# Shifted-window attention block on one core: projections over 128 rows with zero-padded weights, and q and k parts moved straight from tile to tile

## The reference

```python
y = roll(layernorm(x) * w1 + b1, (-3, -3)); win = 7x7 windows of y     # 2048 windows of 49 tokens, 64 channels
q, k, v = split(win @ qkv_w.T)                                          # 8 heads of 8 channels
attn = softmax(q @ k.T * 8**-0.5 + bias + mask)                         # 49 x 49 per window and head
out = (attn @ v) @ proj_w.T + proj_b                                    # windows back, roll back
x = x + out
z = layernorm(x) * w2 + b2
return x + gelu(z @ fc1_w.T + fc1_b) @ fc2_w.T + fc2_b                  # hidden width 256
```

## Time and profile before

| | |
|---|---|
| three timed runs | 2358.63, 2359.13, 2376.8 us (median 2359.13) |
| profiled execution | 2345.75 us, span 2343.9 us |
| mean granted TensorE clock | 0.986 |
| PE, PEld busy | 95%, 72% of the span |
| DVE, ACT, POOL busy | 75%, 66%, 76% |
| DMA | 217.73 MB, mean 93 GB/s; data queue 43.2% of 16 engines |

### The profile page before, as it was taken

How to read it: one execution, slowest core, us unless ns; L and a number is a source line. 1 busy time by engine, 2 the same in 40 slices (tenths; PEclk the granted TensorE clock), 3 DMA queues, 4 the chain that set the end, 5 groups by cost and what they waited for, 6 DMA issues and landing times.

```text
span 2343.9 us, 155989 instructions
## 1 busy us (share of the span) xinstructions
PE 2217.1 (95%) x66852; PEld 1699.0 (72%) x66852; DVE 1756.3 (75%) x3230; ACT 1548.0 (66%) x2435; POOL 1770.1 (76%) x1687
## 2 busy tenths in 40 slices
PE   5999999999999999999999999999999999999997
PEld 4777777777777777777777777777677777777775
DVE  5787787777777877777777777777777777777774
ACT  4567666666666776766666766666666666666765
POOL 5787787777777877776777777777777777777774
PEclk7999999999999999999999999999999999999999
DMA  5444444444444454444444444444444444444541
GB/s 122 98 92 103 91 94 100 87 90 90 95 97 90 96 100 90 99 90 85 96 87 92 102 89 93 103 93 90 94 90 89 93 91 97 94 91 93 103 87 41
DMA packets 137659, 217.73 MB, mean 93 GB/s; under 512 B 29336, under 2 KB 95114, under 8 KB 137114
## 3 DMA queue, kind: packets, MB, share of 16 engines
q1 hardware_dynamic: 137114, 208.95, 43.2%
HBM read 131.69 MB, written 77.15 MB: 89 GB/s over the span
## 4 chain that ended last, share of the span: by engine, by line
PE 85%; ACT 6%; issue 5%; DMA 1%; DVE 1%; POOL 0%; SPq 0%; ACTq 0%; POOLq 0%; DVEq 0%
PE O L759 13%; PE ST L745 11%; PE S L723 9%; PE M L767 9%; PE ST L739 8%; PE M L832 7%; PE M L854 7%; PE M L818 5%; PE M L785 5%; PE M L801 5%; PE M L862 3%; ACT L456 3%; ACT gl L456 2%; PE S L727 2%; DMA xin<-in_x 0%
## 5 line engine op out<-in xcount | busy, mean ns | idle before, releaser
L337 POOL TENSOR_TENSOR nmd<-diag,nm 121x392 f16<-121x392 f16 x1024 | 897.4, 885 | 435.6 <-DVE nm L592 412.5
L592 DVE TENSOR_REDUCE nm<-S 121x8 f16<-121x392 f32 x1024 | 576.7, 563 | 375.9 <-PE S L727 185.0
L437 ACT ACTIVATE pT<-ST 113x392 f32<-113x392 f32 x1024 | 506.2, 495 | 404.7 <-PE ST L745 400.2
L759 PEld LDWEIGHTS O<-vx,pT 113*49 113x49 f32 x16384 | 552.1, 127 | 61.1 <-issue 20.5
L759 PE MATMUL O<-vx,pT 113*49 113x18 f32 x16384 | 530.7, 197 | 16.7 <-issue 14.3
L723 PE MATMUL S<-kp,qp 128*49 128x49 f16 x16384 | 395.6, 186 | 26.4 <-issue 10.7
L739 PE MATMUL ST<-qp,kp 128*49 128x49 f16 x16384 | 396.8, 186 | 23.7 <-issue 22.7
L723 PEld LDWEIGHTS S<-kp,qp 128*49 128x49 f16 x16384 | 318.3, 104 | 100.3 <-issue 75.7
L745 PE MATMUL ST<-nmd,shiftw 121*49 121x392 f16 x2048 | 362.6, 350 | 2.0 <-POOL nmd L337 1.3
L739 PEld LDWEIGHTS ST<-qp,kp 128*49 128x49 f16 x16384 | 330.1, 103 | 37.5 <-issue 27.9
L745 PEld LDWEIGHTS ST<-nmd,shiftw 121*49 121x49 f16 x2048 | 107.1, 101 | 286.4 <-issue 150.0
(11 more groups left out here) (87 smaller groups left out, 3297.6 us busy)
## 6 DMA issues: line engine op xcount, KB each, us to landing
parts<-hl SPq DMA_DIRECT2D x512, 98.0 KB, 2.6
qp<-parts SPq DMA_DIRECT2D x512, 98.0 KB
xin<-in_x SPq DMA_DIRECT2D x256, 98.0 KB
kp<-parts SPq DMA_DIRECT2D x256, 98.0 KB
kp<-parts SPq DMA_DIRECT2D x512, 49.0 KB
out<-res SPq DMA_DIRECT2D x256, 98.0 KB
kp<-in_c_keys SPq DMA_DIRECT2D x4, 588.0 KB, 8.4
weights<-in_c_weights SPq DMA_DIRECT2D x1, 384.0 KB, 3.6
```

What stands on the lines that cost most here:

```text
L337: nc.gpsimd.tensor_tensor(nmd[j % LAG][:], diag[:], nm[j % LAG][:].unsqueeze(2).broadcast_to([RM, 2 * 4, N]), ALU.mult).then_inc(s_nmd, 1)
L437: nc.scalar.activation(pT[j % LAG][:].rearrange("k w h q -> k (w h q)"), ST[0:R, j % 2, 0:HK], ACT.Exp).then_inc(s_e, 1)
L592: V.tensor_reduce(nm[j % LAG][:], S[0:RM, 0:HK].rearrange("q (h n) -> q h n", n=N), AX_X, ALU.max, negate=True).then_inc(s_nm, 1)
L759: mm = MM(O[W0 * w:W0 * w + N, (4 * p + hp) * VC:(4 * p + hp + 1) * VC], pT[j % LAG][:, w, hp, :], vx[r % RING][:, window + w, hp, :], sta ...
```

## The change

project_v and project_out take all 128 rows of the stationary operand in one matmul. The weights are padded with zeros (`apart`), so that the even half's channels give the first 64 (project_v: 32) columns of each result and the odd half's the others. project_v goes from 32 matmuls of 64 rows and 32 columns to 16 of 128 rows and 64 columns; project_out from 8 matmuls of 64 rows, 113 stationary and 64 moving columns to 8 of 128 rows, 49 stationary and 128 moving columns. Each writes one PSUM bank instead of two; `place_v`, `add_attention` and `times_v` read accordingly. M is cleared once at the start. The weights grow from 768 to 896 columns.

The buffer `parts` and both its passes go. `spread_parts` issues 16 transfers a unit, each of 64 pieces of 784 bytes, from `hl` to the rows of qp and kp. SP waits for s_lo and s_sh before the first. `high_parts` now waits for all 16 transfers of the unit before (s_q) instead of the four writes.

```diff
-        wproj = weights[:, 256:320]
+        wproj = weights[:, 256:384]
...
-            def write_parts(u, r):
-                sp.wait_ge(s_lo, u + 1)
-                for b in range(2):
-                    for qk in range(2):
-                        sp.dma_start(parts[r % RING, b, qk].rearrange("s d h t -> (d h) s t"),
-                                     hl[C * qk:C * qk + C, :, b].rearrange("m s a t -> m s (a t)")).then_inc(s_parts[b], 16)
...
-            def read_parts(u, r, b):
-                if b == 0 and later(u, 2):
-                    sp.wait_ge(s_sh, U * u - U)
-                sp.wait_ge(s_parts[b], 32 * u + 32)
-                q, k, landed = qp[r % 2][b], kp[r % 2][b], s_q[r % 2][b]
-                both = [parts[r % RING, b, qk].rearrange("s d h t -> (s d) h t") for qk in range(2)]
-                sp.dma_start(q[BIAS:BIAS + 2 * D], both[0]).then_inc(landed, 16)
-                sp.dma_start(k[BIAS:BIAS + 2 * D], both[1]).then_inc(landed, 16)
-                sp.dma_start(q[BIAS + 2 * D:BIAS + 4 * D], both[0]).then_inc(landed, 16)
-                sp.dma_start(k[BIAS + 2 * D:BIAS + 3 * D], parts[r % RING, b, 1, 1]).then_inc(landed, 16)
-                sp.dma_start(k[BIAS + 3 * D:BIAS + 4 * D], parts[r % RING, b, 1, 0]).then_inc(landed, 16)
+            def spread_parts(u, r, b):
+                if b == 0:
+                    made, read = held(u + 1), held(U * u - U)
+                    sp.wait_ge(s_lo, made)
+                    if later(u, 2):
+                        sp.wait_ge(s_sh, read)
+                q, k = qp[r % 2][b], kp[r % 2][b]
+                for qk, dst, order in ((0, q, (0, 1, 0, 1)), (1, k, (0, 1, 1, 0))):
+                    for n, s in enumerate(order):
+                        part = hl[C * qk:C * qk + C, s, b].rearrange("m a t -> m (a t)")
+                        sp.dma_start(dst[BIAS + D * n:BIAS + D * n + D], part).then_inc(s_q[r % 2][b], 16)
...
-            def high_parts(u):
+            def high_parts(u, r):
                 act.wait_ge(s_qk, u + 1)
                 if later(u):
                     for b in range(2):
-                        act.wait_ge(s_parts[b], 32 * u)
+                        act.wait_ge(s_q[(r + 1) % 2][b], 64 * u + 64 - 64 * ((r + 1) % 2))
...
             V.memset(O[:], 1.0).then_inc(c_blank, 1)
+            V.memset(M[:], 0.0).then_inc(c_blank, 1)
...
             def project_v(u):
                 for s in range(8):
-                    for h in range(2):
-                        for e in range(2):
-                            rows = slice(C * h, C * h + C)
-                            mm = MM(M[W0 * e:W0 * e + N, 2 + h, 32 * s:32 * s + 32], yT[rows, N * s:N * s + N],
-                                    wv[rows, e, :], start=True, stop=True, tile_position=(C * h, W0 * e))
+                    for e in range(2):
+                        mm = MM(M[W0 * e:W0 * e + N, 2, C * s:C * s + C], yT[:, N * s:N * s + N], wv[:, e, :],
+                                start=True, stop=True, tile_position=(0, W0 * e))
...
                 for q in range(4):
-                    for h in range(2):
-                        rows = slice(C * h, C * h + C)
-                        mm = MM(M[0:R, h, C * q:C * q + C], oT[rows, q, :], wproj[rows, :], start=True, stop=True)
+                    for w in range(2):
+                        mm = MM(M[W0 * w:W0 * w + N, 0, 2 * C * q:2 * C * q + 2 * C], oT[:, q, W0 * w:W0 * w + N], wproj,
+                                start=True, stop=True, tile_position=(0, W0 * w))
...
+    def apart(a):
+        a = np.asarray(a).reshape(C, -1, a.shape[-1])
+        both = np.zeros((2, C, a.shape[1], 2, a.shape[2]), np.float32)
+        both[0, :, :, 0], both[1, :, :, 1] = a, a
+        return both.reshape(2 * C, -1)
```

More of the change, by code:

```diff
@@ L37 @@
 NVEC = 23 + SPAN
-NWT = 768
+NWT = 896
 RING = 4
@@ L70, in swin_block @@
         wqk = weights[:, 128:256]
-        wproj = weights[:, 256:320]
-        w1 = weights[:, 320:576]
-        wv = weights[:, 576:640].rearrange("c (e f) -> c e f", e=2)
-        w2 = weights[:, 640:768].rearrange("k (a c) -> k a c", a=2)
+        wproj = weights[:, 256:384]
+        w1 = weights[:, 384:640]
+        wv = weights[:, 640:768].rearrange("c (e f) -> c e f", e=2)
+        w2 = weights[:, 768:896].rearrange("k (a c) -> k a c", a=2)
         st = sb("st", [128, 12, 4])
@@ L118, in swin_block @@
         res = [sb(f"res{r}", [R, UP * C]) for r in range(2)]
-        parts = nc.dram_tensor("parts", [RING, 2, 2, 2, D, HEADS, T], F16, kind="Internal").ap()
         spread = nc.dram_tensor("spread", [HEADS, KEYS, N], F32, kind="Internal").ap()
@@ L159, in swin_block @@
         s_lo = sem("s_lo")
-        s_parts = [sem(f"s_parts{b}") for b in range(2)]
         s_q = [[sem(f"s_q{n}{b}") for b in range(2)] for n in range(2)]
@@ L193, in swin_block @@
         ZEROED = RING + 2
-        BLANK = 3
+        BLANK = 4
         VALUES = 3 * RING
@@ L298, in body @@
                 if on_chip(a):
-                    write_parts(a, m + 1)
-                    read_parts(a, m + 1, 0)
-                    read_parts(a, m + 1, 1)
+                    spread_parts(a, m + 1, 0)
+                    spread_parts(a, m + 1, 1)
                 if isinstance(i, int) and i == -1:
@@ L427, in place_v @@
                     rows = slice(W0 * e, W0 * e + N)
-                    nc.scalar.activation(dst[rows, :, D * e:D * e + D].rearrange("n (a s) d -> n a s d", a=2),
-                                         M[rows, 2:4, 0:256].rearrange("n a (s d) -> n a s d", d=D),
+                    nc.scalar.activation(dst[rows, :, D * e:D * e + D],
+                                         M[rows, 2, :].rearrange("n (s d) -> n s d", d=D),
                                          ACT.Copy).then_inc(s_vx, 1)
@@ L474, in body @@
                     if k == 0 and on_chip(a):
-                        high_parts(a)
+                        high_parts(a, m + 1)
                     if k == 1 and on_chip(a):
@@ L609, in add_attention @@
                 held = xres[r % RING][:].rearrange("r (p h) c -> r p h c", h=2)
-                V.tensor_tensor(held, M[0:R, 0:2, 0:4 * C].rearrange("r h (p c) -> r p h c", c=C), held,
+                V.tensor_tensor(held, M[0:R, 0, :].rearrange("r (p h c) -> r p h c", h=2, c=C), held,
                                 ALU.add).then_inc(s_att, 1)
@@ L713, in scores @@
                 if j % 4 == 0:
-                    pe.wait_ge(s_q[r % 2][b], 80 * (u // 2) + 80)
+                    pe.wait_ge(s_q[r % 2][b], 128 * (u // 2) + 128)
                     if not later(u, 2):
@@ L755, in times_v @@
                     pe.wait_ge(s_on, 2 * u + j // 4)
-                window = 8 * (j % 2) + 4 * (j // 4) + 2 * ((j % 4) // 2)
+                window = 8 * (j // 4) + 4 * ((j % 4) // 2) + j % 2
                 for hp in range(4):
@@ L759, in times_v @@
                         mm = MM(O[W0 * w:W0 * w + N, (4 * p + hp) * VC:(4 * p + hp + 1) * VC],
-                                pT[j % LAG][:, w, hp, :], vx[r % RING][:, window + w, hp, :],
+                                pT[j % LAG][:, w, hp, :], vx[r % RING][:, window + 2 * w, hp, :],
                                 start=True, stop=True, tile_position=(0, W0 * w))
@@ L972 @@
                every(L0_conv_h_times, L0_conv_ws_scalar, L0_conv_ws_scalar2, L0_conv_pow_para), every(line)]
-    matrices = [ident, twice(qkv[0:2].transpose(3, 0, 2, 1)), twice(np.asarray(L0_conv_proj_w).T),
-                twice(np.asarray(L0_conv_fc1_w).T), twice(qkv[2].reshape(4, 2, D, C).transpose(3, 1, 0, 2)),
+    matrices = [ident, twice(qkv[0:2].transpose(3, 0, 2, 1)), apart(np.asarray(L0_conv_proj_w).T),
+                twice(np.asarray(L0_conv_fc1_w).T),
+                apart(qkv[2].reshape(4, 2, D, C).transpose(3, 1, 0, 2).reshape(C, 2, C // 2)),
                 fc2_wT.reshape(128, 2 * C)]
```

## The result

The changed kernel takes 2223.68 us (2222.98 to 2224.8, 4 runs) against 2358.88 (2346.61 to 2376.8, 4 runs) before: ratio 0.9422, 95% interval 0.9361 to 0.9483. That is 135 us less, where the forecast was 71 and the range ended at 2245. The direction was right and the forecast size about half of the measured one.

The account below looks back on a forecast made before the run. PE was taken to bound the kernel, busy 2217.1 of 2343.9 us. Projections 27, fetch 43 and start 5, less gelu 5, gave 70 us: 2276 profiled, 2288 as median, range 2245 to 2345.

Parts of the forecast that it names:

- The projections: On PE, project_v and project_out would each take 0.89 us; 0.07 and 0.14 us a unit saved, together 27 us.
- The second rival: On PE in project_v and project_out, loads of full-height fp32 tiles are not hidden: 62 us slower, 2421; chance 0.05.
- the rule of the Trainium skill: On PE, by streaming alone, two tiles instead of four would add 115 us in all; given no chance.
- The fetch: PE runs out of instructions in the value projection's slot; thinning it saves 40 of 47.7 us, 43 with smaller breaks.
- The moves: Sixteen direct transfers a unit, 7.2 us of issue on SP, 5 us of slack before L418: steady-state cost nothing.
- the first rival: PE's breaks stay, caused by DMA bursts, not density: 2327, or 2343 if denser bursts lengthen them; chance 0.24.
- The start: The first unit's chain through the parts falls from 11.0 to 6.5 us; with clearing M, net 5 us saved.
- The gelu: PE's wait for the gelu at L767, 12.9 us before, grows and takes 5 us back.
- The third rival: The direct q and k moves are slow, at 0.25 us a packet: about 2520; chance 0.04.

Follow-up runs that it names:

- two kernels with the moves and the smaller clearing: The changed kernel with bank 0 of M alone cleared and the transpose of y moved: behind times_v 2263.05 us; between shift and times_v 2213.66 us.

## Why the prediction was right or wrong

**The projections: right.** Forecast 0.89 us each, measured 0.91 and 0.89; 0.21 a unit forecast, 0.22 measured in the clean unit (16.91 to 16.69). The forecast clean unit was 16.7. The parts measured add up to 0.05 + 0.14 = 0.19. The second rival, loads that show, fell: a pair of project_v costs at most 0.91 / 16 = 0.057 us. So did the rule of the Trainium skill (TensorEngine Tiling (Array Packing), Theoretical Speedup) as a forecast for this kernel: the old value projection, in four tiles, held PE for 0.96 us, the new one, in two, for 0.91. What the prediction left open, how much of the old time is the change of tiling, the starts of the matmuls answer: on entering and leaving, the old groups lost 0.18 us each more than the new ones, which is more than the whole gain of the value projection (0.05) and of the output projection (0.14). The output projection was never in four tiles: its old form had two row tiles, its new one has two column tiles.

**The fetch: right in kind, wrong in size. This is the step that failed.** The prediction took "Of the 47.7 us all may go or none", 40 of them, and 43 us in all, 38 with the 5 us that the gelu takes back. It was 100 so counted, or 107 before the gelu's 7. That the value projection's slot is where PE runs out of instructions was right: packets that hold it had 66 of the 98 us. The size came from a row that is too small. The trace of before held the larger number: the earlier trace rows gave a mean unit 0.7 us longer than a clean one, 0.73 x 127 = 93 us, and the prediction said so and then did not use it. Even that is too little, for the last units have less work: the last three periods are 10.7, 7.9 and 5.9 us, before as after, and without them the mean lies some 0.2 us higher. The rows of waits on PE count only idle time between modelled ends of matmuls, and the sum took three of nine rows: all that name issue add up to 64.6 us, where the edges of the packets give 98.

The median moved for the same reason. The prediction put the changed kernel's median 13 us above its profiled execution, as it was before; it was 0.7 above, so the miss is 53 us in the profiled execution and 64 in the median. Before, longer executions tend to have the lower granted clock (among the 13 beside the single changes, 2341 us at 0.987 and 2367 us at 0.978).

**The moves: counted at nothing in the steady state, and that was wrong too.** On PE the slack held: scores waited for a transfer once, at the start. On ScalarE it did not hold always: L407 waited for the moves 12 times behind the start, 27 us in all, where the prediction had it wait for L785 (now L775) alone. But the lighter traffic lets PE's instructions come in time: moves alone brought 58 us, and 36 on top of both projections. The prediction had seen one sign of it (a break just after SP's writes began) and put it into the first rival, with the opposite sign, as denser bursts that could lengthen the breaks. The first rival was half right: a third of the loss at the edges (32 of 98 us) was traffic, and it went because the passes went. The Trainium skill's page (Runtime: NRT & Kernel Launch, Instruction fetch mechanics), by which the fetch is hidden, does not hold here: 99 stops of over 0.3 us stand at the edges of packets.

**The start: wrong sign, small.** Forecast 5 us saved, measured 4.6 lost. The price of an issue, 0.45 us by interpolation, is 0.65, as for 128 pieces. And the prediction let the first eight moves release the chain, 6.5 us; it was all sixteen, for which `high_parts` waits, 14.5 us. The moves alone begin their first turn back at 109.7 us, the two projections alone at 99.2, which speaks for the moves; but two kernels with the moves and the smaller clearing begin at 99.4 and 100.0, and PE's time at half clock before the first turn differs too (61 us with the moves alone, 24 in the one that begins at 99.4), so the size is not separated. The clearing of M cost 1.76 us (1.9 forecast).

**The gelu: about right.** 12.9 us of wait became 19.6, so 7 us instead of the 5 allowed.

The third rival, slow moves, fell: 178074 packets took 28.1% of 16 engines for 2221.2 us, 56 ns each on average.

## What to carry to other kernels

Where an engine's program is fully unrolled, compare the mean period with a clean one and give the whole difference a name before pricing anything: it was 0.7 us of 17.6 here, over three times the 0.22 us by which the clean unit shrank. Stops inside a group that waits for nothing, at a fixed number of instructions apart, were instruction fetch here. Count them by packet: in packets used up in about 2 us they went with fewer instructions in that stretch, in the others with lighter data traffic. Before an extra group is moved in a tuned slot, list what its place covers as well as what it waits for.

## What the runs showed of the hardware that was not expected

- A transfer of 64 pieces from tile to tile took SP 0.65 us to issue (four in 2.60), the same as one of 128 pieces to DRAM (four in 2.55).
- A redundant wait on PE, on a semaphore long reached, cost 78 ns in mean behind project_v, and (2533.6 - 107.8) / 127 - 16.63 = 2.47 us for 64, 39 ns each, behind fc2. Both hold some loss by the clock: in units 5 to 120, PE ran at 0.5 for 642 us in the first run and 133 in the second, with 232 and 62 us lost in those stretches. 64 of them added 16 packets over 128 units, 32 instructions a unit.
- The kernel with breaks varies by 30 us from run to run, the one without by 2: 2346.61 to 2376.8 us before, 2222.98 to 2224.8 after.
- A packet of 256 instructions that PE used up in 2.1 us ended in a stop 44 times of 60, one used up in 4.5 us never as long as the passes through DRAM were gone (0 of 305 in the run with the moves alone).
- Before the change, the granted clock fell to 0.5 behind six of the nine stops of 1.4 us or more, and once without one; these seven stretches were 34 us long in all. After it there was none between the first and the last turn back.
- Entering a group of fp32 matmuls on 64 rows took 0.115 us, entering the new groups on 128 rows 0.02; leaving them 0.14 and 0.19 against 0.05 and 0.10. Together 0.18 us for each group.
